# Feed-forward of four chunks placed inside the integrator's second half, and a first attention that hands scores over by head

## The reference

```python
x = x + ga * _L0_attn_ref(h, ...)          # first layer, block touched by the change
x = x + gb * _L0_ffn_ref(h, ...)           # experts, then a second layer, unchanged

def _forward(x, ...):                      # _L0_attn_ref; H = 16 heads of 8, FF = 512
    xn = _ln(x, g_attn, b_attn)
    qkv = (xn @ qkv_w + qkv_b).reshape(b, s, 3, H, HD)
    ...
    scores = jnp.einsum('bhqd,bhkd->bhqk', q, k) / np.sqrt(HD).astype(np.float32)
    causal = jnp.triu(jnp.ones((s, s), dtype=bool), 1)
    scores = jnp.where(causal[None, None], -jnp.inf, scores)
    attn_w = jax.nn.softmax(scores, axis=-1)
    attn = jnp.einsum('bhqk,bhkd->bhqd', attn_w, v)
    ...
    attn = attn @ out_w + out_b
    x = x + attn
    ctx = attn.reshape(b * s, d)
    xs = _ln(x, g1, b1).reshape(b * s, d)
    vs = jnp.zeros_like(xs)
    def step(carry, _):                    # 8 steps, DT = 0.1
        xs, vs = carry
        u = jnp.tanh(ctx @ w_ctx + xs @ w_x + b_inl)
        vn = vs + DT * (u - xs - vs)
        xn_ = xs + DT * vn
        return ((xn_, vn), None)
    (xs, vs), _ = jax.lax.scan(step, (xs, vs), None, length=NUM_ITERS)
    x = x + xs.reshape(b, s, d)
    h = _ln(x, g2, b2)
    h = jax.nn.gelu(h @ ff_w1 + ff_b1, approximate=False)
    return x + (h @ ff_w2 + ff_b2)
```

## Time and profile before

| what | value |
|---|---|
| runs | 1103.69, 1108.15, 1109.69 us; median 1108.15 |
| profiled execution | 1114.98 us, of which the span of instructions 1113.1 us |
| PE, DVE, ACT, POOL busy | 966.3, 632.2, 553.9, 452.2 us (87, 57, 50, 41%) |
| mean granted clock | 0.935 |
| first attention, row scores alone | about 46 to 77 us |
| first attention, steady | about 77 to 304 us, ends at 334 us |
| integrator, two halves | about 356 to 398 and to 440 us |
| second layer norm, feed-forward | about 438 to 453 and to 509 us |
| experts, second layer | to 1113 us |

### The profile page before, as it was taken

How to read it: one execution, slowest core, us unless ns; L and a number is a source line. 1 busy time by engine, 2 the same in 40 slices (tenths; PEclk the granted TensorE clock), 3 DMA queues, 4 the chain that set the end, 5 groups by cost and what they waited for, 6 DMA issues and landing times.

```text
span 1113.1 us, 21441 instructions
## 1 busy us (share of the span) xinstructions
PE 966.3 (87%) x7366; PEld 612.7 (55%) x7366; DVE 632.2 (57%) x2096; ACT 553.9 (50%) x1077; POOL 452.2 (41%) x681
## 2 busy tenths in 40 slices
PE   6788999999978988999867986799988967989995
PEld 4356666666643222445423885366655522479994
DVE  2658888888814989424613443777754612334443
ACT  4615666666656546636212553467775301235551
POOL 1116776677631999000370552045540271013331
PEclk9859999999998999999888998899999887989998
DMA  6500000000020000300011234000000011001115
GB/s 212 189 1 2 2 2 3 2 2 3 2 85 1 1 1 1 151 1 1 22 53 32 68 106 138 1 1 2 1 1 1 15 53 39 0 18 49 49 36 163
DMA packets 31881, 42.01 MB, mean 38 GB/s; under 512 B 6880, under 2 KB 26720, under 8 KB 30912
## 3 DMA queue, kind: packets, MB, share of 16 engines
q1 hardware_dynamic: 27232, 31.26, 8.9%
q0 software_dynamic: 4544, 9.38, 2.6%
HBM read 29.16 MB, written 16.66 MB: 41 GB/s over the span
## 4 chain that ended last, share of the span: by engine, by line
PE 62%; DVE 17%; ACT 7%; issue 7%; another core or an unknown queue 3%; DMA 2%; DVEq 1%; SPq 1%; POOL 0%; POOLq 0%
PE PS L608 6%; PE PS L399 5%; PE PS L591 4%; PE PS L598 4%; PE PS L303 4%; PE PS L554 4%; PE PS L545 3%; PE PS L547 3%; PE PS L312 3%; DVE PS L1047 3%; PE PS L513 2%; DVE PS L1120 2%; PE PS L508 2%; DVE N L1129 2%
## 5 line engine op out<-in xcount | busy, mean ns | idle before, releaser
L1488 POOL DMA_INDIRECT token_rows<-xnb,slot_in x78 | 75.1, 962 | 196.7 <-ACT xnb L897 190.3
L813 ACT ACTIVATE pw<-PS 128x384 f32<-128x384 f32 x256 | 111.6, 488 | 78.8 <-PE PS L424 76.5
L1425 POOL TENSOR_SCALAR_AFFINE_SELECT pw<-pw 128x256 f32<-128x256 f32 x256 | 104.6, 433 | 95.0 <-ACT pw L813 93.3
L1047 DVE CUSTOM_DVE_ANT_0 PS<-PS,above 128x256 f32<-128x256 f32 x256 | 115.3, 450 | 40.6 <-PE PS L396 38.8
L399 PE MATMUL PS<-kf,qm 32*128 32x256 f32 x512 | 95.4, 450 | 14.3 <-DVE mx L1049 9.6
L1281 DVE TENSOR_TENSOR rsb<-sqb,PS 128x256 f32<-128x256 f32 (+1 forms) x78 | 43.2, 554 | 100.4 <-PE PS L598 59.0
L883 ACT ACTIVATE sqb<-PS 128x512 f32<-128x512 f32 x48 | 28.6, 597 | 142.2 <-PE PS L545 84.4
L1192 DVE TENSOR_TENSOR rsb<-sqb,PS 128x512 f32<-128x512 f32 x48 | 32.9, 687 | 112.8 <-PE PS L547 57.4
L1475 POOL TENSOR_TENSOR XS<-XS,N 128x512 f32<-128x512 f32 x64 | 80.1, 1307 | 28.8 <-DVE N L1120 25.4
L1447 POOL TENSOR_SCALAR_AFFINE_SELECT pw<-pw 128x256 f32<-128x256 f32 x128 | 55.8, 471 | 71.8 <-ACT pw L940 71.8
L1049 DVE CUSTOM_DVE_ANT_0 PS<-PS,above 128x128 f32<-128x128 f32 x256 | 84.6, 331 | 0.0
(11 more groups left out here) (203 smaller groups left out, 2337.8 us busy)
## 6 DMA issues: line engine op xcount, KB each, us to landing
sorted_rows<-empty_rows_dram SPq DMA_DIRECT2D x2, 2535.0 KB, 14.7
slot_in<-sorted_rows SPq DMA_DIRECT2D x78, 65.0 KB
N<-token_rows SPq DMA_DIRECT2D x16, 256.0 KB, 4.8
X<-xT_dram SPq DMA_DIRECT2D x4, 512.0 KB, 6.7
ATT<-gate_dram SPq DMA_DIRECT2D x1, 2048.0 KB
XS<-down_dram SPq DMA_DIRECT2D x1, 2048.0 KB
H<-up_dram SPq DMA_DIRECT2D x1, 2048.0 KB
out_dram<-X SPq DMA_DIRECT2D x8, 256.0 KB, 3.6
```

The source lines that it names most:

```text
L813: nc.scalar.activation(pw[:, w % 2, j + n, :], PS[:, A_PST + (2 * v + n) % 3, 0:3 * P], ACT.Exp).then_inc(a_p, 1)
L1047: nc.vector.tensor_tensor_reduce(x[:, 0:SEQ], x[:, 0:SEQ], above[:, :], 1.0, -3e38, ALU.add, ALU.max, mx[:, 1, j, g:g + 1])
L1425: m = nc.gpsimd.affine_select(x[:, :, SEQ * k:SEQ * k + P], x[:, :, SEQ * k:SEQ * k + P], [[0, 2], [1, P]], ALU.is_ge, 0.0, base=0, channe ...
L1488: nc.gpsimd.indirect_dma_start(token_rows[l][:, :], bass.IndirectOffsetOnAxis(slot_in[:, r, D:D + 1].bitcast(mybir.dt.int32), 0), slot_out ...
```

## The change

Attention: the scores are handed over by head. `row_scores` takes one head: PE waits for the maxima of the head three before, and raises a_s per head; in the step the order is now head 0 high, key scores low, head 1 high, then both low parts. mx has two buffers, the values three. Work of a batch is put on other steps: values projected at u = 3 and stored at u = 4 (before 5 and 6), queries and keys projected at u = 5 (3), their masks at u = 6, 7, 1, 3 (4 to 7), the shuffle at u = 6 (5), the last part of the split maxima between two heads of the next step, and, one batch later than before, the inversion at u = 0 (5), the normalising at u = 2 (6), the output projection at u = 7 (7) and the residual at u = 2 (1). The last two or three batches keep roughly their old places.

Integrator: after the first half the layer norm runs over chunks 0 to 3. Then each pair of q of the second half takes one w1 and one w2 matmul of those chunks between its own: tanh results use two banks (4, 5) instead of four, the w1 result has bank 6, the sum bank 7. The other four chunks follow as before.

```diff
-            def row_scores(t, low):
+            def row_scores(t, n, low):
                 b, g = t // 8, t % 8 // 2
-                if t >= 1 and not low:
-                    pe.wait_ge(a_mx, 2 * t - 1)
-                for n in range(2):
-                    ...
+                j, bank = 2 * (t % 2) + n, (2 * t + n) % 3
+                r = slice(32 * j, 32 * j + 32)
                 if low:
-                    m.then_inc(a_s, 1)
+                    nc.tensor.matmul(PS[:, bank, SEQ:SEQ + P], qm[r, b % 3, g, 0:P], kf[r, b % 3, 0:P],
+                                     start=True, stop=True).then_inc(a_s, 1)
+                else:
+                    ...
+                    if 2 * t + n >= 3:
+                        pe.wait_ge(a_mx, 2 * t + n - 2)
+                    nc.tensor.matmul(PS[:, bank, 0:SEQ], qm[r, b % 3, g, P:SEQ], kf[r, b % 3, :], start=True, stop=True)
...
+        NORM_STEPS = {8 * (b + 3) + 2 if b < BATCH - 2 else 8 * (b + 2) + 6: b for b in range(BATCH)}
+        OUT_STEPS = {8 * (b + 3) + 7 if b < BATCH - 3 else 8 * (b + 3) + 3 if b < BATCH - 2 else 8 * (b + 2) + 7: b
+                     for b in range(BATCH)}
+        INVERT_STEPS = {8 * (b + 3) if b < BATCH - 2 else 8 * (b + 2) + 5: b for b in range(BATCH)}
...
             def maxima(t):
-                dve.wait_ge(a_s, t + 1)
                 for n in range(2):
+                    if n and t % 8 == 0 and t:
+                        last_part(t // 8 - 1)
+                    dve.wait_ge(a_s, 2 * t + n + 1)
...
-            ln(LN_G2, H, settled)
-            for t in range(NCH):
+            for q in range(4 * STEPS):
+                pull(q)
+            ln(LN_G2, H, lambda k: pe.wait_ge(i_h, k + 1), last=NCH // 2)
+            def widen(j):
+                t = j // 4
+                if j % 4 == 0:
+                    pe.wait_ge(ln_out, LNO + 8 * LN_G2 + t + 1)
+                if j:
+                    pe.wait_ge(f_g, j + 4)
+                nc.tensor.matmul(PS[:, F_H, :], w1[:, j % 4 * P:(j % 4 + 1) * P], N[:, t * CH:(t + 1) * CH],
+                                 start=True, stop=True).then_inc(f_h, 1)
+            def narrow(j):
+                if j % 4 == 0:
+                    pe.wait_ge(f_hy, j // 4 + 2)
+                pe.wait_ge(f_g, j + 5)
+                m = nc.tensor.matmul(PS[:, F_Y, :], w2[:, j % 4, :], sqb[:, j % 4, :], start=(j % 4 == 0), stop=(j % 4 == 3),
+                                     skip_group_check=True)
+                ...
+            for j in range(2 * STEPS):
+                pull(4 * STEPS + 2 * j)
+                widen(j)
+                pull(4 * STEPS + 2 * j + 1)
+                narrow(j)
+            ln(LN_G2, H, lambda k: pe.wait_ge(i_h, k + 1), first=NCH // 2)
+            for t in range(NCH // 2, NCH):
...
+            def bend(q):
                 act.wait_ge(i_p, q + 1)
-                if q >= 4:
+                if 4 <= q < 4 * STEPS:
                     act.wait_ge(i_v, q - 3)
-                nc.scalar.activation(PS[:, 4 + q % 4, :], PS[:, q % 4, :], ACT.Tanh, bias=col(C_INL)).then_inc(i_u, 1)
+                elif q >= 4 * STEPS + 2:
+                    act.wait_ge(i_v, q - 1)
+                nc.scalar.activation(PS[:, u_bank(q), :], PS[:, q % 4, :], ACT.Tanh, bias=col(C_INL)).then_inc(i_u, 1)
...
+            for j in range(2 * STEPS):
+                bend(4 * STEPS + 2 * j)
+                gelu(j, F_H)
+                bend(4 * STEPS + 2 * j + 1)
...
+            for q in range(4 * STEPS, STEPS * NCH):
+                if q > 4 * STEPS:
+                    velocity(q - 1)
+                drive(q)
+                if q % 8 == 0 and q >= 4 * STEPS + 8:
+                    feed(q // 8 - STEPS // 2 - 1, F_Y)
```

231 lines of the change are left out of this document (121 added, 110 removed).

## The result

The changed kernel takes 1100.99 us (median of 6 runs, 1096.44 to 1106.57), the kernel before beside it 1108.92 (6 runs). The ratio is 0.993, 95% interval 0.9901 to 0.9958: 7.8 us faster, between 4.7 and 11. The forecast was 17.1 us; less than half came.

What follows compares the result with a forecast made beforehand. It took PE's waits on DVE to bound the attention, DVE the integrator and PE the feed-forward. Gains 5.2 + 8.8 + 3.1 = 17.1 us took 1108.15 to 1091, range 1084 to 1098 (overall 1080 to 1103).

Steps and rivals of the forecast that it cites:

- The row-only stretch: Steps with only row scores: handing over by head shortens the loop from 2.48 to 1.8, gaining 5.2 us.
- between release and DVE's start: Row-only steps: what remains of the loop from PE's release to DVE's start, put at 1.0 us.
- The steady part: Attention batches: three waits of 1.07 go, new ones cost 0.35 and 0.1; 0.6 a batch, 8.8 us gained.
- The wait from the split: Attention, one step before the maxima are transposed: PE's wait for DVE's split maxima, about 0.35 a batch, taken as gone.
- ACT's inversion: Attention, step with the transposes: ACT's logarithm and exponential now stand ahead of it and cost 0.35 a batch.
- Rival (d): Attention: PE begins matmuls strictly in written order, 0.21 more a step, 24.6 us slower, 1116; chance 0.05.
- The integrator: Feed-forward of chunks 0 to 3 inside the integrator's second half: gain 3.1 us, between 6 and -5.
- the first settled chunk is there at 397.6: End of the integrator's first half: last velocity ends at 396.9, first chunk settled at 397.6.
- the low clock that the prediction had seen coming: Layer norm between integrator halves: clock falls after PE's idling, as from 354 to 356 (0.50, after some 3 idle).
- the 0.4 that the forecast added for the table load: Feed-forward after the second layer norm: 0.4 us for the table load ahead of Gelu, beside 27.5 of matmuls.
- The 62.6 of the second half: Integrator's second half: PE-bound, 58.3 us of matmuls plus waits of 2.5 and 1.8, sum 62.6.
- rival (c): Integrator's second half: pairs take 4.1 us, not 3.6, costing 8 us, total 1099; chance 0.12.

Runs made afterwards that it cites:

- e4: Changed kernel with the exponential of the inversion two steps behind its logarithm and normalisation one step later, for the first 13 batches; ratio to the kernel before 0.9964.
- e10: Changed kernel with the first head's low part issued ahead of the second head's high part in every step; ratio to the kernel before 0.9902.
- e15: Changed kernel without the operation that makes the second of the three parts of the maxima; one run, stages sum to 453.3 us.
- e6: Changed kernel with six matmuls that nobody reads added ahead of the first centring after the integrator's first half; ratio to the kernel before 0.9874.
- e5: Changed kernel with POOL's last three additions of the integrator's first half cut to 32 of 512 columns; ratio to the kernel before 0.9896.
- e13: Changed kernel with low parts first in every step, settling through PSUM for two chunks of each half, and two filler matmuls; ratio to the kernel before 0.9857.
- e12: The kernel before, unchanged, run again on a chip of the second group; ratio 0.9991.
- e1: Changed kernel with the old integrator and feed-forward put back, so the attention change alone; ratio to the kernel before 0.9869.
- e3: Changed kernel with each head's low and high row-score parts issued together in steps without key scores; ratio to the kernel before 0.9848.

## Why the prediction was wrong, point by point

**The row-only stretch: right mechanism, mis-sized.** -2.5 instead of -5.2. The term "between release and DVE's start", put at 1.0, was 1.27 (52.40 to DVE's 53.67). The first head's low part had run by 53.20, but its signal came only behind the second head's high part, at 53.65. And the step behind each projection still waited, 0.82 and 0.83, as before. The sum was made from the loop alone and left PE no wait at all: 20.2 for 20.1 of work.

**The steady part: right by number, in part by luck.** -8.2 against -8.8. The batch is 14.83, 0.73 less and not the forecast 0.6, and over the steady batches this gives more than 8.8; but the first batch, in which the clock is at 0.50 for longer than before (to 83.2, before to 80.6), is 1.4 longer (19.1 against 17.7). The prediction had no term for that. The waits for the shuffle and for the normalised heads went. The wait from the split did not: I took it as gone and set 0.35 for ACT's inversion in the same step instead. e4 shows that ACT wasn't the cause of the 2.12, e10 and e15 that the split was; what ACT adds when the split is cured, 0.2 at most, is open. Rival (d) was wrong as a rule for starts: plain steps are 1.71, where 1.71 to 1.77 stood before. Its idea holds for signals, where a head is really held: in the row-only steps and in the step of the transposes.

**The integrator: the step that failed.** "The last velocity so ends at 396.9, and the first settled chunk is there at 397.6": 0.7 was 3.4. This is the first 2.7 us of the miss, and a maximum of 3364 ns stood beside the median in the trace of before. From the first centring on 8.4 were forecast and 9.4 came, with the low clock that the prediction had seen coming but for which it used a row that had only part of it (at 0.50 for 2.9 of the 6.4, against 4.8 us here); with the clock up, in e6, it is 7.2. From the second half's end to the next feed-forward 9.5 were forecast and 10.7 came: the second settling was held again (1.76). The feed-forward behind it took 27.6; the 0.4 that the forecast added for the table load stood in no row, and it doesn't show here. Together with 0.1 in the second half 4.6: forecast -3.1, measured +1.5. The 62.6 of the second half, rival (c)'s place, was right (62.8 by its own terms, since 68 times 0.86 is 58.5, and 62.7 measured): a pair takes 3.62, and one of the three with the stall 4.12.

So of the 7.9 missing between 17.1 and 9.2, 2.7 are the row steps, 4.6 the integrator and feed-forward, nearly all in the two restarts, and 0.6 the steady part.

## What to carry over

Look at the maximum of each line beside its median: an operation that once takes five times its length is held by something, and a change can move it onto the path. A pipeline that is cut in two pays for its end and its start again, and here that was 12.8 us between the halves, with a fallen clock, for 11 us of slack; bridge it with matmuls and keep two-input vector operations away from GpSimd's runs. And hold a gain worked out for a loop against the busiest engine's own work at the clock it has there: a sum that leaves it no wait is a bound, not a forecast.

## What the runs showed of the hardware

**A vector operation with both inputs in SBUF waits for GpSimd's whole run.** The held settling (385.55 to 388.96) outlasted not one addition but three, though two of them began after it, at 385.94 and 387.16: back-to-back additions didn't let it in. With the additions cut short it took 0.68 (e5). It ended 0.55 after the last one in the changed kernel, in e13 and at 405.16 in before (addition to 404.62). With one input in PSUM the same operation took 0.69 in the middle of such a run. The Trainium skill has the port ("SBUF — State Buffer", Who interferes with whom): a vector instruction with two SBUF inputs contends with a GpSimd instruction that reads SBUF, and one with at most one, outside the 2-port modes, doesn't. It also says (same page, SBUF: two separate sides) that whichever starts first has the port for the whole instruction. The trace agrees on the operands. On the order it differs, if the start that the profile shows counts: the two additions that began after the settling went first.

**Matmuls start early, but signal in order.** In the row-only step above the low part ran from 52.41 to 53.20, and its semaphore rose at 53.65, behind the end (53.62) of the high part ahead of it. In e4 the key scores' last pass ended at 209.40, and ACT, which waits for it, started at 209.90, 0.09 after the end of a matmul that stands ahead of it in the program. The Trainium skill's rule that the prediction weighed ("TensorE: Matmul & The Clock Gate", Part 3, The mechanism: begin and end strictly in program order) so holds for the signals in these traces, and not for the starts in the earlier trace rows.

**The clock at a restart differs from one execution to the next.** The column "to half 1" goes from 65.4 over 66.8 to 69.8, in code that no edit touched. The kernel before alone has 66.8 in one execution and 65.4 in the other (e12). The windows from 340 to 348 of e1 (69.8) and of e3 (65.4), whose layer norms ahead of it begin within 0.7 of each other (first centring at 321.42 and 320.78):

```profile
340.00:344.00 4.00, 2.11 (x3) 1.08 (x4) 1.84 (x4) 1.49 (x2) 0.00 (x0) 0.66 0.00 0
344.00:348.00 4.00, 4.00 (x5) 1.45 (x5) 0.69 (x1) 0.66 (x1) 0.83 (x1) 0.50 0.00 0
```

```profile
340.00:344.00 4.00, 4.00 (x10) 1.85 (x11) 0.69 (x1) 0.93 (x2) 0.52 (x1) 1.00 0.00 0
344.00:348.00 4.00, 4.00 (x11) 1.85 (x10) 1.51 (x3) 1.72 (x3) 3.10 (x3) 1.00 0.00 0
```

In both PE idles 3.3 us ahead of the integrator; in one the clock falls to 0.5, in the other it stays. With the layer norm before it, whose clock differs as well, that is 4.4 us, half of what the change is worth. No edit was made there; whether the edits ahead of it set it by shifting the time isn't shown, since each of these kernels has one profile. Why the total of e1 is nearly 6 us better than its stages is left open too: the part behind the feed-forward differs by up to 6.6 us between kernels with the same code there (549.4 in e5, 542.8 in e6).
